# A neuron-model scan on one core: linear part of the first cubic taken apart, clip ahead of the first split, products and terms reordered

## The reference, cut to what matters

```python
def cell(h, x):                       # GRU
    gi, gh = x @ W_ih + b_ih, h @ W_hh + b_hh
    r, z = sigmoid(i_r + h_r), sigmoid(i_z + h_z)
    n = tanh(i_n + r * h_n)
    return (1 - z) * n + z * h

def _derivative(q, p, drive, coupling, bias):
    dq = q - q ** 3 / 3.0 - p + drive + tanh(q) @ coupling.T + bias
    dp = EPSILON * (q + ALPHA - BETA * p)

def _rk4_step(q, p, drive, coupling, bias):      # DT = 0.01, CLAMP = 20
    dq1, dp1 = _derivative(q, p, ...)
    dq2, dp2 = _derivative(q + 0.5 * DT * dq1, p + 0.5 * DT * dp1, ...)
    dq3, dp3 = _derivative(q + 0.5 * DT * dq2, p + 0.5 * DT * dp2, ...)
    dq4, dp4 = _derivative(q + DT * dq3, p + DT * dp3, ...)
    q_next = clip(q + DT / 6 * (dq1 + 2 * dq2 + 2 * dq3 + dq4), -CLAMP, CLAMP)
    p_next = clip(p + DT / 6 * (dp1 + 2 * dp2 + 2 * dp3 + dp4), -CLAMP, CLAMP)
```

## Time and profile before

| | us |
|---|---|
| median of 3 runs | 3536.72 (3535.81 to 3536.73) |
| the profiled execution | 3533.15 |
| its span | 3531.3 |
| TensorE matmuls busy | 3432.0 (97%) |
| weight loads busy | 3162.2 (90%) |
| VectorE busy | 2842.0 (80%) |
| ScalarE busy | 2612.1 (74%) |
| GpSimd busy | 1536.1 (43%) |

### The profile page before, as it was taken

How to read it: one execution, slowest core, us unless ns; L and a number is a source line. 1 busy time by engine, 2 the same in 40 slices (tenths; PEclk the granted TensorE clock), 3 DMA queues, 4 the chain that set the end, 5 groups by cost and what they waited for, 6 DMA issues and landing times.

```text
span 3531.3 us, 297078 instructions
## 1 busy us (share of the span) xinstructions
PE 3432.0 (97%) x115469; PEld 3162.2 (90%) x115469; DVE 2842.0 (80%) x20699; ACT 2612.1 (74%) x23713; POOL 1536.1 (43%) x6169
## 2 busy tenths in 40 slices
PE   8989999999999999999999999999999999999978
PEld 4479999999999999999999999999999999999954
DVE  2068888888888888888888888888888888888876
ACT  3257777777777777777777777777777777777752
POOL 0034444444444444444444444444444444444421
PEclk9999999999999999999999999999999999999978
DMA  3000000000000000000000000000000000000001
GB/s 131 24 26 1 1 1 1 1 1 1 1 1 1 1 1 1 1 1 1 1 1 1 1 1 1 1 1 1 1 1 1 1 1 1 1 1 1 1 2 48
DMA packets 9441, 24.35 MB, mean 7 GB/s; under 512 B 556, under 2 KB 600, under 8 KB 8792
## 3 DMA queue, kind: packets, MB, share of 16 engines
q1 hardware_dynamic: 8832, 19.92, 1.5%
q10 hardware_dynamic: 88, 0.02, 0.0%
HBM read 15.75 MB, written 4.19 MB: 6 GB/s over the span
## 4 chain that ended last, share of the span: by engine, by line
PE 68%; DVE 20%; ACT 7%; issue 5%; DVEq 0%; DMA 0%; ACTq 0%; POOL 0%; POOLq 0%
PE psum L1193 38%; PE psum L1150 23%; PE psum L1120 5%; DVE tpart L857 4%; ACT tpart L582 4%; DVE psum L902 2%; ACT tfull L584 2%; DVE qnext L902 2%; DVE psum L888 2%; DVE psum L874 2%; PE psum L1296 1%; DVE q L909 1%; DVE psum L867 1%; DVE gates L791 1%; DVE psum L892 1%
## 5 line engine op out<-in xcount | busy, mean ns | idle before, releaser
L1193 PE MATMUL psum<-tpart,cpl 128*128 128x32 f16 (+1 forms) x65536 | 1965.9, 175 | 30.7 <-DVE tpart L857 11.1
L1193 PEld LDWEIGHTS psum<-tpart,cpl 128*128 128x128 f16 x65536 | 1781.3, 96 | 144.5 <-DVE tpart L857 54.9
L1150 PE MATMUL psum<-hpart,whh 128*128 128x32 f16 x49152 | 1554.1, 176 | 17.8 <-DVE hpart L833 11.4
L1150 PEld LDWEIGHTS psum<-hpart,whh 128*128 128x128 f16 x49152 | 1375.0, 96 | 26.9 <-DVE hpart L833 18.8
L857 DVE TENSOR_TENSOR tpart<-tfull,tpart 128x8 f16<-128x8 f32 x4096 | 675.1, 165 | 226.6 <-ACT tfull L584 94.5
L582 ACT ACTIVATE tpart<-psum 128x8 f16<-128x8 f32 x3072 | 518.4, 175 | 157.7 <-DVE psum L902 91.5
L902 DVE TENSOR_REDUCE psum<-psum 128x8 f32<-128x24 f32 x3072 | 548.7, 190 | 73.2 <-issue 4.0
L584 ACT ACTIVATE tfull<-psum 128x8 f32<-128x8 f32 x3072 | 520.2, 176 | 0.0
L582 ACT ACTIVATE tpart<-qnext 128x8 f16<-128x8 f32 x1024 | 213.3, 208 | 319.5 <-DVE qnext L902 319.5
L546 ACT ACTIVATE qterm<-psum 128x16 f32<-128x16 f32 x3072 | 390.2, 179 | 78.7 <-DVE psum L880 5.4
L392 POOL TENSOR_TENSOR pterm<-pterm,uhat 128x48 f32<-128x48 f32 x512 | 146.3, 286 | 527.3 <-ACT pterm L553 527.3
(11 more groups left out here) (153 smaller groups left out, 4324.5 us busy)
## 6 DMA issues: line engine op xcount, KB each, us to landing
xrow<-in_x_dram SPq DMA_DIRECT2D x4, 1024.0 KB, 12.0
out_dram<-space SPq DMA_DIRECT2D x16, 256.0 KB, 2.0
wih<-in_L_cond_W_ih_dram SPq DMA_DIRECT2D x3, 1024.0 KB, 10.8
space<-in_L_cond_W_hh_dram SPq DMA_DIRECT2D x1, 3072.0 KB, 20.0
space<-in_L_cond_coupling_dram SPq DMA_DIRECT2D x1, 1024.0 KB, 19.2
xrow<-in_cond_dram SPq DMA_DIRECT2D x1, 1024.0 KB, 4.4
wih<-in_L_cond_Wk_dram SPq DMA_DIRECT2D x1, 1024.0 KB, 5.2
wih<-in_L_cond_Wo_dram SPq DMA_DIRECT2D x1, 1024.0 KB, 8.3
```

Of the source, the lines that this page charges most:

```text
L1150: mm = pe.matmul(gate_out[x][:, :, :, c * B:(c + 1) * B], whh[:, w, k, n * P:(n + 1) * P], copies_in(hpart[:, k, :, :]), start=(c == 0 and ...
L1193: mm = pe.matmul(stage_out[a][:, 0:reps, :, col:col + B], cpl[:, w, k, n * P:(n + 1) * P], copies_in(tpart[:, s % 2, k, :, :])[:, 0:reps, ...
```

## The change: what it does, and the diff

- In stage 0 `shift_square` is gone. `linear` computes `linear0 = drive0 - STEP[3]/3 * LINEAR[0] * q1`, `cubic(0)` is min(square, 400) times q1 in one instruction that reads the square itself, and `base(0)` adds `linear0` and not `drive0`. VectorE has as many instructions as before.
- The clip stands ahead of half A's split, not behind it.
- TensorE issues 10 matmuls behind half A's split and not 12, so that half A's output is complete after 18; the two others come behind it.
- ScalarE's `stage_terms` of stages 0 and 1 stand right behind half B's tanh, ahead of the square, and wait for no cubic.
- VectorE's `argument(0)` stands between the sums of stage 1 and not ahead of them; `new_high(0)` and `new_h_full(0)` stand ahead of `cubic(2)`.
- Waits that other waits or an engine's order cover are left out: on `omzs_ready` in `weigh`, on `ka_read` in `new_high` from v = 3 on, on `qterm_ready` in `cubic(3)` and in the sums of stages 1 and 2.

```diff
...
-        cub, square0, lowest = [psum[:, scratch_at + i * KB:scratch_at + (i + 1) * KB] for i in range(3)]
+        cub, lowest = [psum[:, scratch_at + i * KB:scratch_at + (i + 1) * KB] for i in range(2)]
...
-                    if s == 2:
-                        stage_terms(2)
+                    if s < 3:
+                        stage_terms(s)
                     arg, s_next = (in_halves(qnext[:, :]), 0) if s == 3 else (qt, s + 1)
...
                             sigmoids(0, gru)
-                        act.wait_ge(cub_ready, stage_count(1, now))
-                        stage_terms(0)
-                        if gru <= T:
                             scaled_omz(0, gru)
...
                             scaled_drive(tail)
-                        act.wait_ge(cub_ready, stage_count(2, now))
-                        stage_terms(1)
                         if gru <= T:
...
                 dve.wait_ge(cand_ready[x], v)
-                dve.wait_ge(omzs_ready[x], v)
...
-                    if x == 0:
+                    if x == 0 and v <= 2:
                         dve.wait_ge(ka_read, v)
...
-            def shift_square(v):
-
-                dve.wait_ge(sq_ready[0], v - 1)
-                dve.tensor_scalar(square0, sq[:, 0, :], CLAMP * CLAMP, LINEAR[0], ALU.min, ALU.add).then_inc(shift_ready, 1)
+            def linear(v):
+
+                dve.wait_ge(q1_ready, v)
+                dve.wait_ge(drive0_ready, v)
+                dve.scalar_tensor_tensor(linear0[:, :], q1[:, :], -STEP[3] / 3 * LINEAR[0], drive0[:, :],
+                                         ALU.mult, ALU.add).then_inc(linear_ready, 1)
...
-                    dve.wait_ge(shift_ready, v)
+                    dve.wait_ge(sq_ready[0], v - 1)
                     dve.wait_ge(q1_ready, v)
-                    dve.tensor_tensor(cub, square0, q1[:, :], ALU.mult).then_inc(cub_ready, 1)
+                    dve.scalar_tensor_tensor(cub, sq[:, 0, :], CLAMP * CLAMP, q1[:, :], ALU.min, ALU.mult).then_inc(cub_ready, 1)
                 else:
 
                     dve.wait_ge(sq_ready[s], v)
-                    if s == 3:
-                        dve.wait_ge(qterm_ready[s], v)
...
-                    dve.wait_ge(drive0_ready, v)
-                    dve.scalar_tensor_tensor(stage_base, in_halves(cub), -STEP[3] / 3, in_halves(drive0[:, :]),
+                    dve.wait_ge(linear_ready, v)
+                    dve.scalar_tensor_tensor(stage_base, in_halves(cub), -STEP[3] / 3, in_halves(linear0[:, :]),
...
                     dve.wait_ge(base_ready, stage_count(s, v))
-                    if s in (1, 2):
-                        dve.wait_ge(qterm_ready[s], v)
...
                     reset(0, gru)
+
+                sum_stage(1, 0, now)
+                if gated_step:
                     argument(0, gru)
-
-                sum_stage(1, 0, now)
                 sum_stage(1, 1, now)
                 split_tanh(2, 0, now, tanh_ready[1][0], now)
                 if gated_step:
                     weigh(0, gru)
                 split_tanh(2, 1, now, tanh_ready[1][1], now)
-                cubic(2, now)
                 if gated_step:
                     new_high(0, gru)
                     new_h_full(0, gru)
+                cubic(2, now)
                 base(2, now)
...
                 sum_stage(3, 1, now)
+                clip(now)
                 if tail <= T:
                     split_tanh(0, 0, tail, tanh_ready[3][0], now)
-                clip(now)
-                if tail <= T:
                     split_tanh(0, 1, tail, tanh_ready[3][1], now)
-                    shift_square(tail)
+                    linear(tail)
                     cubic(0, tail)
                     base(0, tail)
...
                     pe.wait_ge(t_parts[s][0], now)
-                    stage_products(s, k_first, range(HK + 1))
+                    stage_products(s, k_first, range(HK))
+                    stage_products(s, k_first[:1], [HK])
                     pe.wait_ge(t_parts[s][1], now)
                     stage_products(s, k_second, range(HK)).then_inc(stage_mm[s][0], 1)
+                    stage_products(s, k_first[1:], [HK])
                     stage_products(s, k_first, range(HK + 1, K))
                     stage_products(s, k_second, range(HK, K)).then_inc(stage_mm[s][1], 1)
...
```

More of the change, by code:

```diff
@@ L126, in build @@
         qnext = sb("qnext", [P, KB])
+        linear0 = sb("linear0", [P, KB])
         q1 = sb("q1", [P, KB])
@@ L268, in build @@
         qterm_ready = [sem(f"qterm_ready{s}") for s in range(4)]
-        pterm_ready, shift_ready = sem("pterm_ready"), sem("shift_ready")
+        pterm_ready, linear_ready = sem("pterm_ready"), sem("linear_ready")
         cub_ready = sem("cub_ready")
@@ L915, in _ @@
                                    condT[:, :, :].rearrange("p k b -> p (k b)"), ALU.mult))
-            dve.tensor_scalar(square0, sq[:, 0, :], LINEAR[0], None, ALU.add).then_inc(shift_ready, 1)
-            cubic(0, 1)
+            linear(1)
+            dve.tensor_tensor(cub, sq[:, 0, :], q1[:, :], ALU.mult).then_inc(cub_ready, 1)
             base(0, 1)
```

## The result

The changed kernel takes 3559.78 us (median of 4 runs, 3559.54 to 3560.58) where the kernel before, timed beside it, takes 3536.26 (3535.68 to 3536.73). The ratio is 1.007, with a 95% interval of 1.0059 to 1.0082: it is slower by 0.7%, some 24 us. The forecast was 3558, slower.

A forecast was written before the change was run, and what follows sets the result against it. The step was taken as a loop of latencies through the engines; stages of -0.19, +0.08, +0.10 and +0.07 gave 6.20 against 6.14 us, +31 us, less 10 for pauses: 3554 profiled, 3558 as median, range 3538 to 3574.

The forecast's parts named there:

- What bounds the kernel: Whole step: TensorE waits in every stage; products, sum, tanh, split, products form a loop, 6.14 us a clean step before.
- Split base: Stage 0: without the shift the 0.16 us that the base cost is gone; 1.40 against 1.59, a gain of 0.19.
- Clip ahead of split A: Step's start on VectorE: split A follows the clip by 0.14 us, 0.11 later than now; the clip comes 0.12 earlier.
- Terms ahead of the square: Stage 1: three Copies, 0.19 us, delay square 1, cubic, base and sum A; the stage takes 1.59, 0.08 more.
- New h and two terms in stage 2: Stage 2: cubic 2 becomes third of three VectorE slots, the square stays covered; the stage takes 1.63, 0.10 more.
- Argument and ten matmuls: Stage 1's argument: candidate's tanh pays nothing but has no room; ten matmuls: no price, up to 0.05 a stage uncovered.
- Waits removed: Six waits, covered by other waits or engine order: nothing, at most 0.02 us a step.
- Sum: Whole run: 0.06 us a clean step, +31 us, less 10 for pauses: 3554 profiled, 3558 as the runs' median.
- Pauses: Stretches where an engine waits for nothing: 34 us in all before, of which 10 were to come back.
- (a): Rival, stage 1: square 1 doesn't set base 1, the recovered base shows through; -61 us, 3476; chance 0.1.
- (c): Rival, step's start: split A waits until the clip is through, 0.225; +42 us, 3600; chance 0.04.

The follow-up runs named there:

- the fastest one: The kernel before with the split base, argument(0) between stage 1's sums and argument(1) behind half A's split of stage 3: 3457.69 us, ratio 0.9803.

## Why the prediction was right, point by point

**What bounds the kernel.** Right for the changed kernel. The loop of latencies, stage by stage, gave 1.40, 1.59, 1.63 and 1.58; the medians of the trace are 1.40, 1.63, 1.61 and 1.58. The clean step was to be 6.20; it is 6.22. For the kernel before one reading was wrong: half A's sum of stage 1 was not held by the argument in front of it but by the wait for stage 0's recovery terms. The number survived, because the changed kernel's stage 1 was worked out from its base and not from that reading.

**Split base.** Right, and shown alone: -60 us, 0.12 us a step. The stage 0 that the prediction gave to it as a gain of 0.19 holds the clip's share as well.

**Clip ahead of split A.** The slot of 0.14 was right to the row, and so was the price in stage 3, 0.07 (0.07 to 0.08 in all three pairs of kernels). What the pairs differ in is what stages 0 and 1 do with a block that starts later: stage 0 gives back 0.07, 0.05 or 0.11, stage 1 takes 0, 0.04 or 0.04 (clip alone; with the split base; in the changed kernel). In time: nothing, 31 us, 18 us.

**Terms ahead of the square.** Right in kind: square 1 ends last and holds cubic 1, base 1 and stage 1's sum. Stage 1 was counted 0.04 too short, mostly since the square took 0.23 us behind the Copies where I had used 0.20. What the prediction did not see is that these terms had held the sum from behind the cubic before, so that moving them ahead took one wait away and put another in its place.

**New h and two terms in stage 2.** Right in kind, and the largest single loss, 50 us by the ratios and 61 to 69 by the same chip and the clean step (the expectation said 44). Which of the two it was is not separated.

**Argument and ten matmuls.** Right: no price for the ten. The argument's move is good in the changed kernel (105 us against its undoing) and worth nothing in the kernel with the split base, where the recovery terms hold the sum.

**Waits removed.** They were not tried by themselves. One of them, the sum's wait for the recovery terms, was the one that ended last in stage 1 of the kernel before; in the changed kernel the terms are done long before the base, so its removal itself gives nothing that the trace shows.

**Sum.** The clean step went up by 0.077 us and not by 0.06, 39 us in place of 31. Pauses had been counted at 34 us before, with 10 of them given back; on the changed kernel they are (6.274 - 6.220) x 511 = 28, so 6 came back. That makes +33 in the scan against a forecast of +21, 12 too little. Against that stand the part outside the scan, 5.5 shorter in the profiled execution (4.9 of it behind the last clip), and the median of the runs, which had been put 3.6 above the profiled execution and lies 0.8 below it. The time forecast, 3558, lies 1.8 below the measured 3559.8 because these fell together with opposite signs. The direction and the stages were worked out; the last 10 us are luck.

**Rivals.** The recovered base did not show through in the changed kernel, but it does once the terms, the clip and stage 2 are taken back: 18, 22 and 50 us one by one, 83 together (1.007 to 0.9835, with the ten and the waits). It was decided where (a) said: square 1 does set base 1. Split A did not wait for the clip's end, it started 0.14 behind the start of an operation of 0.23. The Trainium skill's rule in (c), of the page "VectorE: DVE Perf Modes", section "The DRAIN you can't avoid", would have made that 0.23; it did not here. The rival took only half of that section of the Trainium skill: it adds that a next operation which isn't held starts earlier, and the 0.14 agrees with that. No run here shows a held one.

## What to carry to other kernels

Where every stage of a loop waits for a chain through several engines, lay the chain out once with starts from a clean step, and follow a change through all of it: the gain is what the last path moves, and a good edit next to two bad ones looks like a bad change. Move an operation ahead of another only if its slot isn't on the path that ends last *after* the change. Undo each part from the changed kernel and add each part to the old one: the same edit was worth nothing in one and 31 us in the other. And don't take the operation in front of a late one for what holds it: set its start against the end of everything it waits for, over many steps. The distance that stays the same is the wait that ends last.

## What the runs showed of the hardware that I had not expected

- ScalarE's square took longer behind three Copies issued close before it: 0.23 where it was 0.20 before. In the clean steps the three Copies take 0.191, 0.203 and 0.215 in the median and the square 0.228, each 0.012 or 0.013 longer than the one in front of it.
- VectorE's argument took 0.30 in one order and 0.22 in another. GpSimd's sum ran beside it in both. The cause is open.
- Half A's sum waits for several semaphores, and only one wait is its own; the others stand in front of it as entries (VectorE's program has 20699 operations in both kernels, but 29457 entries in the trace of the kernel before and 28432 in the changed one's). It starts 0.13 behind the end of ScalarE's terms where these come last (0.129 to 0.131 in nine of ten steps of the kernel before) and 0.10 behind the end of VectorE's own base where that does, while cubic 1, which waits for the square alone, starts 0.03 behind its end. What makes the difference was not tried.
- The pauses have a place. Between 300 and 3300 us VectorE has 104 idle stretches in the kernel before that no wait explains, 23.6 us together and 0.35 at the longest, and every one stands, to within one, at a 128th instruction of its program (waits counted); in the changed kernel there are 83, 17.4 us together, at the same places. ScalarE has none.
- The mean step exceeds the median one by less in the changed kernel and least where the argument holds both sums: 6.210 against 6.143 before, 6.274 against 6.220, 6.471 against 6.433. That longer waits swallow more of the pauses fits these three and the shorter sum of idle stretches above. It isn't a rule of all kernels here: in the fastest one it is 6.073 against 6.018.
